# Last attention sums with the gathered rows as TensorE's weights and scaled one-hot blocks as the moving operand

## What is computed

```python
ex    = exp(alpha - amax[dst])                      # one number per edge and head
denom = segment_sum(ex, dst)                        # per node and head
attn  = ex / (denom[dst] + 1e-16)
out   = segment_sum(attn[:, :, None] * v[src], dst) # v = h @ Wv + bv, 4 heads of 128
out   = out.mean(axis=1)                            # mean over the heads
skip  = h @ Wskip + bskip
beta  = sigmoid(concat([out, skip, out - skip]) @ Wbeta)
out   = beta * skip + (1 - beta) * out              # then graph norm, gelu, residual
```

## Time and profile before

| | |
|---|---|
| median of three runs | 6823.21 us |
| the profiled execution, its own time | 6831.6 us |
| its span | 6829.8 us |
| stage s3, TensorE's first to last matmul | 4852.63 to about 5579.3 us |
| end stage, TensorE's work on the tiles | 5589.09 to about 5650.8 us |
| busy shares of the whole span: PE, DVE, ACT, POOL | 68%, 46%, 26%, 66% |

### The profile page before, as it was taken

One profiled execution on the slowest core, in us unless ns is written; L12 is line 12 of the kernel. 1 busy time (PEld: TensorE's weight loads), 2 busy tenths in 40 slices (PEclk: granted clock), 3 DMA queues, 4 the chain that ended last, 5 costly groups with the idle time before them and its releaser, 6 DMA issues. The chain is left out here.

```text
span 6829.8 us, 84212 instructions
## 1 busy us (share of the span) xinstructions
PE 4610.6 (68%) x20762; PEld 4030.5 (59%) x20763; DVE 3115.2 (46%) x6433; ACT 1782.8 (26%) x5141; POOL 4526.1 (66%) x4579
## 2 busy tenths in 40 slices
PE   2899999754333367777776777776699993333334
PEld 2899999734333346666666666665588883333334
DVE  3444444433222233333335888887677774111113
ACT  1222222010000013333333444454466651000000
POOL 4777777047777737777772777775477744777772
PEclk7555555576555577777778999998799996555556
DMA  3333333042222132222222555555222211111111
GB/s 95 100 101 101 103 101 103 21 152 60 64 63 57 53 109 59 59 58 58 59 55 79 157 157 157 157 157 150 76 77 74 77 42 47 51 52 51 52 51 32
DMA packets 266377, 568.61 MB, mean 83 GB/s; under 512 B 89346, under 2 KB 138361, under 8 KB 265433
## 3 DMA queue, kind: packets, MB, share of 16 engines
q0 software_dynamic: 130688, 271.45, 16.2%
q1 hardware_dynamic: 135510, 294.82, 12.6%
HBM read 471.19 MB, written 101.55 MB: 84 GB/s over the span
## 5 line engine op out<-in xcount | busy, mean ns | idle before, releaser
L1418 PE MATMUL PS<-arena,att 128*128 x3328 | 741.2, 414 | 1229.8 <-DMA arena<-tab_h,HT 634.0
L911 PE MATMUL PS<-arena 128*128 128x258 f32 (+1 forms) x4992 | 1322.5, 432 | 259.8 <-ACT arena L869 242.9
L1418 PEld LDWEIGHTS PS<-arena,att 128*128 128x128 f32 x3328 | 689.0, 316 | 1283.7 <-issue 1283.7
L911 PEld LDWEIGHTS PS<-arena 128*128 128x128 f32 x4992 | 1085.0, 220 | 475.2 <-issue 266.1
L1076 POOL DMA_INDIRECT arena<-tab,idx_src x832 | 857.0, 1030 | 323.0 <-issue 252.2
L1367 POOL DMA_INDIRECT arena<-tab_rel,HT x782 | 756.4, 967 | 470.7 <-issue 238.1
L528 PE MATMUL PS<-arena 128*128 x3328 | 820.1, 402 | 237.8 <-DVE arena L588 228.5
L1367 POOL DMA_INDIRECT arena<-tab_h,HT x782 | 768.0, 982 | 300.3 <-issue 238.0
L389 POOL DMA_INDIRECT arena<-tab_rel,arena x832 | 793.2, 953 | 251.0 <-issue 225.7
L389 POOL DMA_INDIRECT arena<-tab_x,arena x832 | 787.8, 947 | 255.5 <-issue 251.4
L528 PEld LDWEIGHTS PS<-arena 128*128 128x128 f32 x3328 | 644.5, 199 | 413.2 <-issue 315.7
(11 more groups left out here) (334 smaller groups left out, 5128.4 us busy)
## 6 DMA issues: line engine op xcount, KB each, us to landing
arena<-drel_rows SPq DMA_DIRECT2D x208, 512.0 KB
spill<-arena SPq DMA_DIRECT2D x104, 516.0 KB
arena<-spill SPq DMA_DIRECT2D x104, 516.0 KB
tab_rel<-arena SPq DMA_DIRECT2D x50, 512.0 KB
arena<-tab,idx_src POOLq DMA_INDIRECT x832
arena<-tab_rel,arena POOLq DMA_INDIRECT x832
arena<-tab_x,arena POOLq DMA_INDIRECT x832
arena<-tab_rel,HT POOLq DMA_INDIRECT x782, 2.5
```

The lines of the kernel that those rows point to most:

```text
L911: ins = nc.tensor.matmul(PS[:, b:b + wc], M[q % 2][:, k * P:(k + 1) * P], rhs, start=(g == 0), stop=(g == 1))
L1418: ins = nc.tensor.matmul(acc, M[s % RM][:, k * P:(k + 1) * P], G[:, bass.ds(e * (2 * D) + g * D, D)], start=False, stop=True, skip_group_c ...
```

## The change

A new stage `stage_attend` takes the place of s3, and the end stage is written anew for its layout.

```diff
+        def stage_attend(spill):
+            RG, DEN = 7, 3584
+            HD = 4 * P
...
+                    def onehots(s):
+                        if s >= 2:
+                            dve.wait_ge(sum_done, 4 * (s - 1))
+                        for k in range(8):
+                            c = 8 * s + k
+                            ins = dve.tensor_scalar(M[s % 2][:, k * P:(k + 1) * P], iota_row[:], drel[:, c:c + 1], None,
+                                                    ALU.is_equal)
+                        ins.then_inc(m_done, 1)
...
+                    for s in range(SETS):
+                        if s + 1 < SETS:
+                            onehots(s + 1)
+                        tiles = load_tiles(mybir.EngineType.DVE, ntile, s * 4, NT - 1)
+                        for u, n in enumerate(tiles):
...
+                            nc.vector.tensor_tensor(a, a, PS[:, b:b + HD], ALU.add).then_inc(add_done, 1)
...
+                        pool.wait_ge(m_done, s + 1)
+                        weights(s, 0, 2, 4)
+                        weights(s, 2, 2, 4)
+                        weights(s, 4, 1, 2).then_inc(wp_done, 1)
...
+                        act.wait_ge(m_done, s + 1)
+                        for k in range(4, 8):
+                            for h in range(2 if k == 4 else 0, 4):
+                                c = (8 * s + k) * 4 + h
+                                ins = nc.scalar.activation(W[s % 2][:, k, h, :], M[s % 2][:, k * P:(k + 1) * P], ACT.Copy,
+                                                           scale=att[:, c:c + 1])
+                        ins.then_inc(wa_done, 1)
...
+                        pe.wait_ge(full[s % NQ], 16 * (s // NQ + 1))
+                        pe.wait_ge(wp_done, s + 1)
+                        for u, n in enumerate(tiles):
...
+                                nc.tensor.matmul(PS[:, bass.ds(n * 4 + DEN, 4)], M[s % 2][:, k * P:(k + 1) * P],
+                                                 att[:, c:c + 4], start=False, stop=True, skip_group_check=True)
+                                x = ((s % NQ) * 8 + k) * 129
+                                ins = nc.tensor.matmul(PS[:, b:b + HD], G[:, x:x + D],
+                                                       W[s % 2][:, k, :, :].rearrange("p h d -> p (h d)"),
+                                                       start=(g == 0), stop=(g == 1))
```

In the end stage the four turns of each tile go, and so do `normalise` and the copy of the turned blocks. The sums already stand with the feature in the partition, and are the weights of four matmuls against Wv, each into its own columns:

```diff
-                                ins = nc.tensor.transpose(PS[:, b:b + P],
-                                                          a4[:, a, h // 2, (h % 2) * D:(h % 2) * D + D], ident[:])
...
+                                ins = nc.tensor.matmul(PS[:, b:b + D], ACC[:, a * 512 + h * P:a * 512 + (h + 1) * P],
+                                                       wv[:, h * D:(h + 1) * D], start=True, stop=True)
...
+                            for h in range(4):
+                                b = (a % 2) * 512 + h * D
+                                ins = nc.scalar.activation(parts[a % 2][:, h * D:(h + 1) * D], PS[:, b:b + D], ACT.Copy,
+                                                           scale=rd[:, 4 * a + h:4 * a + h + 1])
...
+                            nc.scalar.copy(parts[c % 2][:, 512:640], PS[:, b:b + D]).then_inc(s_uf, 1)
...
+                            dve.tensor_reduce(OUT[:, c * D:(c + 1) * D],
+                                              parts[c % 2].rearrange("p (h f) -> p f h", h=5), AX_X, ALU.add
+                                              ).then_inc(s_oe, 1)
```

More of the change, by code:

```diff
@@ L1768, in stage_transformer_end @@
             gt, sg = A[:, o + 200:o + 225], A[:, o + 232:o + 257]
[L1769 to L1774, removed]
+            parts = [A[:, o + 260 + 640 * i:o + 900 + 640 * i] for i in range(2)]
+            aT = [A[0:4, o + 1540 + P * i:o + 1668 + P * i] for i in range(2)]
+            TM = [A[:, o + 1796 + 256 * i:o + 2052 + 256 * i] for i in range(2)]
+            assert o + 2308 <= ARENA
+            den = PS[:, 3584:3584 + 4 * NT]
             with nc.Block() as block:
@@ L1790, in _ @@
                     pe.wait_ge(s_w, 160)
+                    pe.wait_ge(s_ra, 1)
                     for a in range(NT + 1):
                         if a < NT:
[L1793 removed]
                             if a >= 2:
[L1795 removed]
+                                pe.wait_ge(s_ue, a - 1)
                                 pe.wait_ge(s_ae, a - 1)
[L1797 to L1801 removed]
                             b = 1024 + (a % 2) * 512
                             nc.tensor.transpose(PS[0:4, b:b + P], ra[:, 4 * a:4 * a + 4], ident[:]).then_inc(s_at, 1)
+                            for h in range(4):
+                                b = (a % 2) * 512 + h * D
+                                ins = nc.tensor.matmul(PS[:, b:b + D], ACC[:, a * 512 + h * P:a * 512 + (h + 1) * P],
+                                                       wv[:, h * D:(h + 1) * D], start=True, stop=True)
+                            ins.then_inc(s_u, 1)
                         if a > 0:
@@ L1806, in _ @@
                             if c >= 2:
-                                pe.wait_ge(s_oe, c - 1)
+                                pe.wait_ge(s_uf, c - 1)
                                 pe.wait_ge(s_ske, c - 1)
[L1809 to L1812, removed]
+                            b = (c % 2) * 512
+                            nc.tensor.matmul(PS[:, 3072 + b:3072 + b + D], HT[:, c * P:(c + 1) * P], wsk, start=True,
+                                             stop=True)
                             pe.wait_ge(s_ae, c + 1)
[L1814 to L1817, removed]
+                            nc.tensor.matmul(PS[:, 2048 + b:2048 + b + D], aT[c % 2], bv, start=True, stop=True
+                                             ).then_inc(s_o, 1)
                     pe.wait_ge(s_ske, NT)
@@ L1847, in _ @@
                     ch = Chain("t_c", dve)
-                    den = a4[:, :, :, 256:258]
-                    ch(dve.tensor_scalar(r4, den, 1e-16, None, ALU.add))
+                    ch(dve.tensor_scalar(rd, den, 1e-16, None, ALU.add))
                     ch(dve.reciprocal(rd, rd))
                     ch(dve.tensor_scalar(rd, rd, 0.25, None, ALU.mult))
[L1852 to L1861, removed]
+                    dve.tensor_tensor(ra, den, rd, ALU.mult).then_inc(s_ra, 1)
                     dve.wait_ge(s_w, 160)
@@ L1865, in _ @@
                     ch(dve.tensor_tensor(wb2, wb2, wb3, ALU.subtract))
[L1866 to L1870, removed]
-                            dve.wait_ge(s_o, c + 1)
[L1872 to L1877, removed]
+                    for a in range(2, NT + 4):
+                        if a <= NT + 1:
+                            c = a - 2
+                            dve.wait_ge(s_o, c + 1)
+                            b = 3072 + (c % 2) * 512
+                            dve.tensor_tensor(SK[:, c * D:(c + 1) * D], PS[:, b:b + D], bsk, ALU.add).then_inc(s_ske, 1)
+                            dve.wait_ge(s_ue, c + 1)
+                            dve.wait_ge(s_uf, c + 1)
+                            dve.tensor_reduce(OUT[:, c * D:(c + 1) * D],
+                                              parts[c % 2].rearrange("p (h f) -> p f h", h=5), AX_X, ALU.add
+                                              ).then_inc(s_oe, 1)
+                        if 3 <= a <= NT + 2:
+                            c = a - 3
                             dve.wait_ge(s_ske, c + 1)
@@ L2175, in build @@
         end_stage()
-        ACC = stage_aggregate("s3", (0, NT * 516), [258, 258], heads=4, spill=spill2, width=129)
+        ACC = stage_attend(spill2)
         end_stage()
```

94 lines of the change are left out of this document (81 added, 13 removed).

## The result

The changed kernel takes 7011.7 us, the median of four runs (7009.61 to 7015.53), where the kernel before takes 6822.05 us on the same chip. The ratio is 1.0279, 95% interval 1.0264 to 1.0294: slower by 189.7 us. Forecast were 6996 us, +173.

The account below looks back on a forecast made before the run. TensorE's records were taken to bound the sums, before and after. Sums +170, start -2 and end stage +5 gave +173 on 6823.2, so 6996 us; own range 6968 to 7041, widened to 6965 to 7060.

Parts of the forecast that it names:

- TensorE in the sums: Sums stage: TensorE's block goes from 0.8696 to 1.074 us over 832 blocks, +170 us (ends +152 and +195).
- open load: Sums: a weight load with only a 4-column record above it, two per block, taken at 0.110 us each.
- long record: Sums: a TensorE record of 512 columns, two per block, taken at 0.427 us each.
- The rule of the skill: Sums: the notes' claim that weight loads are pulled ahead and cost nothing, giving about 0.90 us per block.
- The clock: TensorE's granted clock in the sums: forecast to stay 1.00 though half the records are short.
- third rival: Sums: short records drop TensorE's clock to 0.50, a block costs 2.13 us, near 7880 us; chance 0.05.
- The chain: Sums: VectorE's add and one-hots, then GpSimd's products, 7.1 to 8.1 us per set, covered by TensorE's 8.59.
- The first rival: Sums: the VectorE and GpSimd chain becomes the bound, 9.3 us per set, 73 us over forecast, 7069; chance 0.11.
- The second rival: Sums: M's loads hide and the chain sets the time, +15 to +120 us, near 6893; chance 0.05.
- The start: Start of the sums: first one-hots come before ACC's clearing, so TensorE starts earlier; -2 us (ends -5 and +3).
- The end stage: End stage's 25 tiles: 2.55 us per tile instead of 2.22, +5 us (ends -6 and +20).
- The ring: End stage: ScalarE's scaling and VectorE's reduction wait on each other over two buffers of `parts`, 2.55 us per tile.

Follow-up runs that it names:

- e1: Changed kernel without the 4-column matmuls (attention's denominators left out): 6835.82 us, ratio to the kernel before 1.0028; the sums stage lasts 730.3 us.
- e4: Kernel before with its 516 columns split as 512 and 4 instead of 258 and 258, nothing turned: 6992.84 us, ratio 1.0257.
- e2: Changed kernel with each 4-column matmul issued twice: 7195.73 us, ratio to the kernel before 1.0554; stage 1089.5 us.
- e9: Changed kernel with four buffers for the head parts in the end stage instead of two: ratio to the kernel before 1.0202.
- e6: Changed kernel with one more GpSimd product of 1024 elements per set: stage 926.2 us against 901.0, ratio to the kernel before 1.026.
- e7: Changed kernel with two more GpSimd products of 768 elements per set: stage 978.4 us against 901.0, ratio to the kernel before 1.032.
- e3: Changed kernel with its small matmuls moving 128 columns instead of 4: 7002.54 us, ratio to the kernel before 1.0273; stage 901.5 us.
- e5: Changed kernel with bf16 one-hots and ex as two bf16 parts, one small record instead of two: stage 809.1 us, ratio to the kernel before 1.0127.
- e10: Kernel before with the stage's first one-hot blocks built ahead of the clearing of ACC instead of behind it: 6823.98 us, ratio 1.0.

## Why the prediction was right

The mechanism of the forecast is the one that ran, and the time lies in its range. By its own steps:

- **TensorE in the sums.** Forecast 1.074 us per block and +170; measured 1.081 and +175. The 0.110 per open load was 0.11, the 0.427 per long record 0.43. The step carried because the pattern was read where it already stood, in another stage at half clock, and scaled by the clock. e1 to e4 show it, by the length of the sums: without the small matmuls 4 us are left of the loss; twice as many, twice the loss; 32 times the columns, the same loss; the same split without the turn, the same loss. That the price is the load's, as the forecast has it, and not a short record's own, is argued from the rows, and the number does not depend on it.
- **The rule of the skill.** The Trainium skill, TensorE: Matmul & The Clock Gate, "Step-by-step: what each phase is for", has the weight loads pulled ahead of running matmuls. By that rule the forecast's estimate was 0.90 us per block, and e2 would have cost little; the block took 1.081 and e2 cost 188.5 us. In these runs a load starts with the record ahead of it (5206.65 and 5207.30 above) and hides under that one only: with two short records in a row, both loads show.
- **The clock.** It stayed 1.00 in the sums, as forecast, with half of the records short ones: the third rival had no part. In the end stage it did fall, to 0.78 on the mean, with TensorE busy for 44.03 of 54.00 us; what stands under e9 shows that this cost about half a microsecond. Why the first layer stays at 0.50 is open.
- **The chain.** Forecast 7.1 to 8.1 us; by e1, e6 and e7 it takes about 7.2, and it was covered. GpSimd's products ran at 1.90 us, as alone, though VectorE's adds lay beside them. The forecast priced a chain that is too long wrongly, at its whole excess in every set; the runs show half of it. The first rival's 73 us would have been about 37 by the same terms, (9.3 - 8.59) / 2 x 104, so near 7033, well inside the forecast's range. The second rival's +15 to +120 halve in the same way.
- **The start.** Forecast -2, measured +4.6, outside its ends of -5 and +3. The step failed where it let GpSimd's products run at 1.9 us beside the clearing, as the earlier trace rows had them; the first took 15.2 us, so TensorE started at 4847.78, 18.0 us behind the end of the first one-hots, where the forecast has 4.4.
- **The end stage.** Forecast +5, measured +9.8, within its ends. The ring was right; its term for the reduction was mis-sized. I had 0.79 us for 640 elements, from the slope between two different instructions, L1884 (an elementwise one over 128 columns) and L1889 (a reduction of 256 neighbours to one sum); it took 1.25, about 1.95 ns per element. The ring took 2.76 us per tile instead of 2.55.

The 16.7 us by which the forecast was short are these: 5 in the sums, 7 at the start, 5 in the end stage. All three terms erred to the same side, and the start's lay outside its ends; the range, made wide by the sums and the end stage, took that in. Its own lower end is 6964 by its terms (152 - 5 - 6 on 6823.2), not 6968.

## What to carry to other kernels

Count records and their weight loads, not only columns: in these runs each f32 record with a fresh 128-column load cost at least 0.11 us at full clock, so a matmul of 4 columns beside one of 512 costs what 128 columns would (e3), while the even split of the kernel before hides every load. Where such a small product is needed, make it a single bf16 record (e5), or let it move up to 128 columns for the same price. With two buffers, price a chain that is longer than the bounding engine's set at half its excess. And look for the same pattern elsewhere in the program at any clock before pricing a new one.

## What was not expected of the hardware

- A VectorE reduction that makes 128 sums of five elements which lie 128 apart took 1.25 us for 640 elements (L1980), where one sum over 256 neighbours takes 0.409. No run separates the distance from the number of sums.
- GpSimd's products of 1024 elements take 1.90 us beside VectorE's adds with one operand in PSUM (L1383). In the kernel before the two products of a set (L826, 5210.99 and 5212.86) took 1.9 and 2.89 us; the second started while L935, with both operands in SBUF, was running, and L935 took 2.62 us there and 2.36 for two without a product beside it (5211.36 and 4851.27).
- A GpSimd product that starts in the 2.62 us in which VectorE stands still ahead of clearing 12800 columns, or just at their edge, ends only behind the clearing (15.2 us in the changed kernel, 13.77 in e3, 12.17 for 256 elements in e5). One that starts 0.45 us after such a clearing has begun was not held (e10).
